# Scans two at a time in odd steps, the sums of squares moved behind the output part of step 1

## What is computed

```python
xn = layernorm(x)
gate, xBC, dt = split(xn @ in_proj_w.T, [8192, 8192 + 10240])      # 128 heads of 64
xBC = silu(causal_conv4(xBC) + conv_b)
xs, B, C = split(xBC)                                              # 8 groups of 16 heads
dt = clip(softplus(dt + dt_bias), 0.001, 100)
y = ssd(xs, B, C, D, dt)     # chunks of 128: (C B^T * exp(cs_l - cs_s) masked) @ (xs dt) + xs D
yg = y * silu(gate)
out = yg * rsqrt(mean_over_group(yg**2) + eps) * norm_w
s = out @ out_proj_w.T
g = silu(moe(xn))            # 16 experts of 56, top 2
return x + s * g
```

## Time and profile before

| | |
|---|---|
| median of 3 runs | 1604.44 us |
| the profiled execution, its own time | 1603.83 us |
| its span | 1602.0 us |
| TensorE's granted clock | 0.999 of full |
| busy PE, DVE, ACT, POOL | 1587.9, 1406.6, 1199.9, 959.6 us |

### The profile page before, as it was taken

How to read it: one execution, slowest core, us unless ns; L and a number is a source line. 1 busy time by engine, 2 the same in 40 slices (tenths; PEclk the granted TensorE clock), 3 DMA queues, 4 the chain that set the end, 5 groups by cost and what they waited for, 6 DMA issues and landing times.

```text
span 1602.0 us, 28468 instructions
## 1 busy us (share of the span) xinstructions
PE 1587.9 (99%) x8478; PEld 1266.6 (79%) x8478; DVE 1406.6 (88%) x1654; ACT 1199.9 (75%) x2309; POOL 959.6 (60%) x600
## 2 busy tenths in 40 slices
PE   9999999999999999999999999999999999999998
PEld 6888777887778777887778777887778777877776
DVE  7727899889999899889999899889998899889987
ACT  5525878777787878777787878777887878778772
POOL 6522466655666656655666556655666566656563
PEclk9999999999999999999999999999999999999999
DMA  5234344334443344334443334334433334334432
GB/s 188 80 131 150 127 138 169 115 132 142 146 146 112 128 137 165 118 131 143 141 146 117 127 130 168 122 130 144 145 141 119 126 129 166 126 120 152 152 132 86
DMA packets 83832, 216.89 MB, mean 135 GB/s; under 512 B 10576, under 2 KB 12880, under 8 KB 83536
## 3 DMA queue, kind: packets, MB, share of 16 engines
q1 hardware_dynamic: 83376, 214.55, 39.3%
q10 hardware_dynamic: 288, 0.30, 0.1%
HBM read 209.83 MB, written 4.98 MB: 134 GB/s over the span
## 4 chain that ended last, share of the span: by engine, by line
PE 84%; DVE 7%; ACT 4%; issue 3%; POOL 1%; DMA 0%; ACTq 0%; DVEq 0%; POOLq 0%
PE pj L455 15%; PE pj L457 14%; PE pj L456 14%; PE pr L455 9%; PE pr L456 8%; PE pr L457 7%; PE sc L702 7%; PE sc L706 3%; PE tb L691 3%; DVE conv L1394 3%; ACT decay L984 1%; DVE decay L1422 1%; DVE xc L1408 1%; DVE wo_lo L1458 1%; PE pr L680 1%
## 5 line engine op out<-in xcount | busy, mean ns | idle before, releaser
L1096 POOL TENSOR_TENSOR w_lo<-stg,w_hi 128x512 fp32r<-128x512 f32 x316 | 494.9, 1567 | 315.1 <-ACT w_hi L958 254.4
L455 PE MATMUL pj<-xT_hi,w_hi 128*128 128x512 f32 x1208 | 476.5, 394 | 3.6 <-POOL w_lo L1096 1.5
L457 PE MATMUL pj<-xT_hi,w_lo 128*128 128x512 f32 x1208 | 470.8, 390 | 0.0
L456 PE MATMUL pj<-xT_lo,w_hi 128*128 128x512 f32 x1208 | 470.4, 389 | 0.0
L1394 DVE SCALAR_TENSOR_TENSOR conv<-pj,par,conv 128x510 f32<-128x510 f32 (+2 forms) x480 | 357.8, 745 | 77.0 <-ACT conv L966 63.6
L984 ACT ACTIVATE decay<-decay,dtg 128x256 f32<-128x256 f32 (+1 forms) x1024 | 379.0, 442 | 0.0
L1137 POOL TENSOR_TENSOR xc<-xc,thg 128x512 f32<-128x512 f32 x128 | 203.1, 1587 | 188.9 <-DVE xc L1445 188.6
L1143 POOL TENSOR_TENSOR sqsum<-sqsum,sq 128x512 f32<-128x512 f32 x112 | 216.7, 1935 | 115.4 <-ACT sq L1012 112.1
L455 PEld LDWEIGHTS pj<-xT_hi,w_hi 128*128 128x128 f32 x1208 | 226.7, 188 | 58.8 <-issue 8.5
L457 PEld LDWEIGHTS pj<-xT_hi,w_lo 128*128 128x128 f32 x1208 | 226.7, 188 | 48.2
L456 PEld LDWEIGHTS pj<-xT_lo,w_hi 128*128 128x128 f32 x1208 | 226.9, 188 | 45.3
(11 more groups left out here) (185 smaller groups left out, 1976.4 us busy)
## 6 DMA issues: line engine op xcount, KB each, us to landing
stg<-wstream SPq DMA_DIRECT2D x387, 256.0 KB, 2.7
decay<-cs_scr SPq DMA_DIRECT2D x128, 768.0 KB, 4.3
acc<-hid SPq DMA_DIRECT2D x8, 256.0 KB, 5.0
out<-acc SPq DMA_DIRECT2D x8, 256.0 KB, 2.0
dt_scr<-decay SPq DMA_DIRECT2D x1, 1024.0 KB, 5.7
gate_scr<-part SPq DMA_DIRECT2D x4, 256.0 KB, 2.0
dtg<-dt_scr SPq DMA_DIRECT2D x16, 64.0 KB, 4.1
stg<-hid SPq DMA_DIRECT2D x4, 256.0 KB, 4.9
```

The lines of the kernel that those rows point to most:

```text
L455: nc.tensor.matmul(dst, hi_w, hi_x, start=first, stop=False)
L456: nc.tensor.matmul(dst, hi_w, lo_x, start=False, stop=False)
L457: return nc.tensor.matmul(dst, lo_w, hi_x, start=False, stop=last)
L1096: nc.gpsimd.tensor_tensor(w_dest(n, 1), stg[:, s % RING, :], f32(w_dest(n, 0)), ALU.subtract).then_inc(S["wl"], 1)
```

## The change

Each pair's scan used to stand in its own step. Now even steps hold none, and odd step s holds `scan(s-1)` and `scan(s)` next to each other; the transposes stay one per step. Each of the two needs a bank: pairs 0, 2, 4, 6 write `sc`; pair 1 writes `tb`, pair 3 `pr[0]`, pairs 5 and 7 `pr[3]`, with waits on those who used these banks last (`acc` of add_output, `u` of add_scan). The sums of squares go behind the output part of step 1, into `sc`, and the transposes of pair 2 go behind them. On VectorE both add_scans stand in the odd step, and both block_weights (s and s+1) and both y_lo in the even one; ScalarE's y_hi and square go in twos in even steps, its drops and decays are for s+1 and no longer for s+2; GpSimd does all weight splits of a step first, then the squares, and both `gated` in odd steps. SyncE issues the exponents of two pairs in even steps.

```diff
@@ banks
...
+        yb = [sc, tb, sc, pr[0], sc, pr[3], sc, pr[3]]
@@ SyncE, step
 def step(g, half, s):
...
-    if has_pair(g, half, s + 3):
-        load_exponents(*pair(g, half, s + 3))
+    for n in (s + 2, s + 3):
+        if s % 2 == 0 and has_pair(g, half, n):
+            load_exponents(*pair(g, half, n))
@@ TensorE
 def x_turn(g, half, j):
...
-    pe.wait_ge(S["ms"], at(g, half, 1, 0 if j >= 2 else -1))
...
+    if j == 2:
+        pe.wait_ge(S["u"], at(g, half, NJ, 2))
@@ TensorE, scan
 def scan(g, half, j):
...
-    pe.wait_ge(S["u"], at(g, half, NJ, j))
+    pe.wait_ge(S["u"], at(g, half, NJ, j - 1))
+    if j == 2:
+        pe.wait_ge(S["ms"], at(g, half, 1, 0))
+    if j > 1 and j % 2 == 1:
+        pe.wait_ge(S["acc"], at(g, half, 4, 1 if j == 3 else 4))
+    if j == 5:
+        pe.wait_ge(S["fg"], NTT)
...
-            nc.tensor.matmul(sc[hd, c0:c0 + 2 * P], xdt[:, j % 2, 2 * b, hd],
+            nc.tensor.matmul(yb[j][hd, c0:c0 + 2 * P], xdt[:, j % 2, 2 * b, hd],
...
-            mm = nc.tensor.matmul(sc[hd, c0 + P:c0 + 2 * P], xdt[:, j % 2, 2 * b + 1, hd],
+            mm = nc.tensor.matmul(yb[j][hd, c0 + P:c0 + 2 * P], xdt[:, j % 2, 2 * b + 1, hd],
...
 def square_sums(g, half):
...
-    pe.wait_ge(S["xdt"], at(g, half, NJ, 0 if isinstance(g, int) and g == G else 2))
+    if isinstance(g, int) and g == G:
+        pe.wait_ge(S["xdt"], at(g, half, NJ, 0))
+        dst = tb
+    else:
+        pe.wait_ge(S["u"], at(g, half, NJ, 1))
+        dst = sc
...
-        mm = nc.tensor.matmul(tb[:, t:t + 1], sqsum[:, t * P:(t + 1) * P], ones, start=True, stop=True)
+        mm = nc.tensor.matmul(dst[:, t:t + 1], sqsum[:, t * P:(t + 1) * P], ones, start=True, stop=True)
@@ TensorE, out_first
...
+    if t in (0, 3):
+        pe.wait_ge(S["u"], at(g, half, NJ, 4 if t == 0 else NJ))
@@ TensorE, step
...
-    if s == 1 and with_out:
-        square_sums(g, half)
...
-    if has_pair(g, half, s + 1):
+    if s != 1 and has_pair(g, half, s + 1):
         x_turn(*pair(g, half, s + 1))
-    if has_pair(g, half, s):
+    if s % 2 == 1 and has_pair(g, half, s):
+        scan(g, half, s - 1)
         scan(g, half, s)
...
     if with_out:
         out_of_step(g, half, s)
+    if s == 1 and with_out:
+        square_sums(g, half)
+    if s == 1:
+        x_turn(*pair(g, half, s + 1))
@@ ScalarE, step
...
 def step(g, half, s, with_out=True):
...
+    before = (g, 0) if half == 1 else (g - 1, 1)
...
+    gated = ("g", s) in blocks(g, half, s)
+    mine = [b[1] for b in blocks(g, half, s) if b[0] == "x"]
+    todo = list(range(len(pieces(g, half, s))))
+    raised = has_pair(g, half, s + 1)
+    done = []
+    if s == 0 and with_out:
+        done = [(*before, NJ - 2), (*before, NJ - 1)]
+    elif s >= 2 and s % 2 == 0 and has_pair(g, half, s - 1):
+        done = [(g, half, s - 2), (g, half, s - 1)]
+    if gated and todo:
+        split(g, half, s, todo.pop(0))
+    if raised and not fill:
+        drops(*pair(g, half, s + 1), 0)
+    if gated:
         gate_tanh(g, half, s)
...
+    if done:
+        y_hi(*done[0])
+    if mine:
+        tap(g, half, mine[0])
+    if todo:
+        split(g, half, s, todo.pop(0))
     if fill and s == 4:
         expert_hi(13)
...
+    if done:
+        y_hi(*done[1])
+        square(*done[0])
+    if raised and fill:
+        drops(*pair(g, half, s + 1), 0)
+    if raised:
+        drops(*pair(g, half, s + 1), 1)
+    if raised and s % 2 == 1:
+        decays(*pair(g, half, s + 1))
...
+        x_tanh(*of_half(g, half, mine[0]), mine[0])
+    for m in mine[1:]:
+        tap(g, half, m)
+    if todo:
+        split(g, half, s, todo.pop(0))
+    if raised and s % 2 == 0:
+        decays(*pair(g, half, s + 1))
+    for m in mine[1:]:
+        x_tanh(*of_half(g, half, m), m)
+    if done:
+        square(*done[1])
+    while todo:
+        split(g, half, s, todo.pop(0))
@@ ScalarE, the end
...
-y_hi(G - 1, 1, NJ - 1)
-square(G - 1, 1, NJ - 1)
+for j in (NJ - 2, NJ - 1):
+    y_hi(G - 1, 1, j)
+    square(G - 1, 1, j)
@@ GpSimd, step
...
-    if with_out and s == 0:
-        add_square(*before, NJ - 1)
+    for i in range(1, n):
+        split_low(g, half, s, i)
     if with_out and s == 2:
         inverse_rms(*before)
-    if s >= 2 and has_pair(g, half, s):
+    if s >= 4 and s % 2 == 0 and has_pair(g, half, s):
+        add_square(g, half, s - 2)
+    if with_out and s == 0:
+        add_square(*before, NJ - 2)
+        add_square(*before, NJ - 1)
+    if s >= 2 and s % 2 == 0 and has_pair(g, half, s):
...
-    for i in range(1, n):
-        split_low(g, half, s, i)
-    if has_pair(g, half, s):
+    if s % 2 == 1 and has_pair(g, half, s):
+        gated(g, half, s - 1)
@@ GpSimd, the end
...
+add_square(G - 1, 1, NJ - 2)
@@ VectorE, add_scan
...
-                                   in1=sc[:, :], op0=ALU.mult, op1=ALU.add).then_inc(S["u"], 1)
+                                   in1=yb[j][:, :], op0=ALU.mult, op1=ALU.add).then_inc(S["u"], 1)
@@ VectorE
 def mean_square(g, half):
...
-    nc.vector.tensor_scalar(msq[:, :], tb[:, 0:4], 1.0 / (GH * HD), 4.0 * EPS, ALU.mult, ALU.add
+    sums = tb if is_last(g, half) else sc
+    nc.vector.tensor_scalar(msq[:, :], sums[:, 0:4], 1.0 / (GH * HD), 4.0 * EPS, ALU.mult, ALU.add
@@ VectorE, step
 def step(g, half, s, with_out=True):
...
+    fill = isinstance(g, int) and g < 0
...
+    even = s % 2 == 0
+    done = []
+    if s == 0 and with_out:
+        done = [(*before, NJ - 2), (*before, NJ - 1)]
+    elif s >= 2 and even and has_pair(g, half, s - 1):
+        done = [(g, half, s - 2), (g, half, s - 1)]
...
     if half == 1 and s == 4 and not isinstance(g, int):
         conv_parameters(g + 1)
...
+    if with_out and s == 2:
...
+    if with_out and s == 5:
+        add_output(*before, 3)
     if has_pair(g, half, s):
         gate_silu(g, half, s)
...
+    if mine:
...
+    if fill and s == 4:
         expert_weighted(13)
     if s == 5 and not is_last(g, half):
         mask_products(*following(g, half))
...
+    if even and has_pair(g, half, s + 1):
         x_times_dt(*pair(g, half, s + 1))
...
+    if not even and has_pair(g, half, s):
+        add_scan(g, half, s - 1)
         add_scan(g, half, s)
+    if not even and s != 1 and has_pair(g, half, s + 1):
+        x_times_dt(*pair(g, half, s + 1))
+    if even and has_pair(g, half, s):
+        block_weights(g, half, s)
...
+    if fill and s == 4:
         expert_lo(13)
...
+    if done:
+        y_lo(*done[0])
     if mine:
         x_silu(*of_half(g, half, mine[0]), mine[0])
...
+    if even and s != 4 and has_pair(g, half, s + 1):
+        block_weights(g, half, s + 1)
+    for m in mine[1:]:
+        x_silu(*of_half(g, half, m), m)
+    if with_out and 3 <= s <= 4:
+        add_output(*before, s - 2)
+    if not fill:
         split_out_lo(g, half, s)
...
+    if s == 4 and has_pair(g, half, s + 1):
+        block_weights(g, half, s + 1)
+    if with_out and s == 2:
+        add_output(*before, 0)
+    if s == 1 and has_pair(g, half, s + 1):
+        x_times_dt(*pair(g, half, s + 1))
+    if done:
+        y_lo(*done[1])
@@ VectorE, the end
...
+y_lo(G - 1, 1, NJ - 2)
+finish(4)
...
-finish(4)
...
```

More of the change, by code:

```diff
@@ L1014, in step @@
             def step(g, half, s, with_out=True):
-                mine = [b for b in blocks(g, half, s) if b[0] == "x"]
-                n = len(pieces(g, half, s))
-                i = 0
+                before = (g, 0) if half == 1 else (g - 1, 1)
                 fill = isinstance(g, int) and g < 0
[L1019 to L1026, removed]
-                    if has_pair(g, half, s + 2):
-                        drops(*pair(g, half, s + 2), 0)
-                    gate_tanh(g, half, s)
-                elif has_pair(g, half, s + 2):
-                    drops(*pair(g, half, s + 2), 0)
@@ L1032, in step @@
-                if s >= 1 and has_pair(g, half, s - 1):
-                    y_hi(g, half, s - 1)
-                    square(g, half, s - 1)
-                if s == 0 and with_out:
-                    before = (g, 0) if half == 1 else (g - 1, 1)
-                    y_hi(*before, NJ - 1)
-                    square(*before, NJ - 1)
-                if has_pair(g, half, s + 2):
-                    drops(*pair(g, half, s + 2), 1)
-                if mine and not (fill and s == NJ - 1):
-                    tap(g, half, mine[0][1])
@@ L1043, in step @@
-                if i < n:
-                    split(g, half, s, i)
-                    i += 1
+                gated = ("g", s) in blocks(g, half, s)
[7 more added lines that the diff above has]
+                    done = [(g, half, s - 2), (g, half, s - 1)]
@@ L1046, in step @@
+                if gated and todo:
[3 more added lines that the diff above has]
+                if gated:
+                    gate_tanh(g, half, s)
+                if done:
[4 more added lines that the diff above has]
+                    split(g, half, s, todo.pop(0))
                 if fill and s == 4:
                     expert_hi(13)
```

(51 more changed lines are left out.)

2 lines of the change are left out of this document (removed).

## The result

The changed kernel takes 1646.64 us (median of 4 runs, 1643.4 to 1650.15), the kernel before 1605.26 us beside it (1604.13 to 1606.73). The ratio is 1.0257, 95% interval 1.0243 to 1.027: 2.6% slower, where 0.7% faster was forecast. The profiled execution has a span of 1643.5 us, 41.5 more than before.

What follows compares the result with a forecast made beforehand. TensorE, busy 99% of the span, was taken to set the time. From 1603.8 us, 23 us of gross gain off and 12 us of new waits for VectorE added gave 1592.8, stated as 1592.5; range 1580 to 1608.

Steps and rivals of the forecast that it cites:

- The gross gain, 23 us: TensorE: scans in twos save 21.8 us over 64 pairs of steps, moved sums of squares 1.2; together about 23.
- the sum without waits: Rival "no new waits": all of VectorE's room holds and TensorE never waits; 1581, up to 1585 us; chance 0.22.
- The rival on the switch: TensorE's second scan pays as the first does: 9.6 us less gain, 1602 with waits, no change; chance 0.10.
- I cost both at nothing: SyncE's two pairs of exponents in even steps, and piece loads queued behind them, needed a step later: 0 us.
- the forecast's net gain of 11: Whole kernel: 23 us gross gain less 12 us of waits, 1603.8 to 1592.8 us.
- Waits for VectorE, 12 us with a bound of 33: TensorE waiting at scans of pairs 3 and 5 after VectorE-GpSimd collisions: 0.8 us a half, 12 in all; bounds 0 and 33.
- Pair 5 was to wait in half 0: scan(5) behind add_output(3): TensorE's 14.5 us against VectorE's 13.6, room 0.9; one and a half collisions overrun it by 0.75.
- split_out_lo was costed at 0.66: VectorE's split_out_lo, start to start, 0.66 us in the sums of room for pairs 3 and 5.
- the room of 0.9: Pair 3, half 0: TensorE's 10.5 us against VectorE's 9.6; one collision of 1.1 overruns it by 0.2.
- out_second(0) for y_lo(7): 0.1 to 0.3 allowed: Remaining waits, such as y_lo(7) ahead of out_second in half 1 and exp of s+1: 0.1 to 0.3 us.
- 0 to 1.5 us allowed for the last step: Kernel's end: y_hi, square and y_lo of two pairs behind the last scans, the first covered by 24 products; 0 to 1.5 us.
- VectorE becomes the bound: Rival: scan(5) and scan(3) wait for add_output after collisions, 2.0 us a half, 31 us, 1612, slower; chance 0.16.

Runs made afterwards that it cites:

- tiny_squares: Changed kernel with exponents of one pair loaded each step and GpSimd's add_square cut to 4 of 512 columns, so squares are not summed: 1581.65 us, 0.9853.
- one_load: Changed kernel with SyncE loading the exponents of one pair (s+2) in each step instead of two pairs in even steps: 1624.06 us, 1.0126.
- late_finish: Changed kernel with VectorE's calls of `finish` in the last step moved behind what TensorE waits for: 1641.2 us, 1.0222.
- squares_before_splits: Changed kernel with one load a step and the first of an even step's two add_squares back ahead of the later weight splits on GpSimd: 1658.2 us, 1.0331.

## Why the prediction was wrong, step by step

**The gross gain, 23 us: right.** Transposes to scan 0.53, two scans 2.75, transposes to products 0.35, sums of squares 0.81 (in tiny_squares, where they don't wait): each within 0.02 of its term, but for the transposes behind the sums of squares, 0.39 and not 0.36. The second scan costs 1.30, not 1.45. tiny_squares ends at 1581.65, where the sum without waits gave 1581, and its loop gains 2.9 us an iteration. The rival on the switch falls.

**"I cost both at nothing", of the exponents' loads: the step that failed most.** The prediction asked who needs the data and found room of a step. It did not ask what else goes through the same DMA engines at that time: the loop ends in step 4, an even one, right behind the loads, and the packets of code that the branch waits for are on nobody's list of instructions. The term is 22.6 us (one_load), by itself more than the forecast's net gain of 11. With it at 22.6 and nothing else changed, the sum would have been 1615, slower. It could have been read from the trace of before: six branches of 3.9 to 4.3 us with 0.4 us uncovered each, so that nothing was left there to give.

**Waits for VectorE, 12 us with a bound of 33: mis-sized.** one_load against tiny_squares gives 42 us: 3.5 for each iteration of the loop, and 15 behind it. The mechanism was right: collisions with GpSimd lengthen block_weights and y_lo by 1.1 each, and the squares are the cause. The Trainium skill, page SBUF — State Buffer, section SBUF: two separate sides, calls the port pair an exclusive lock; the rows agree: a y_lo of 0.68 becomes 1.76, and the ends of both rows add up as turns. Five errors made up the size.

- Places. The largest recurring wait, Q for add_scan(0), 15 x 0.67 = 10 us, isn't among the deadlines at all, though the diff shows it, `pe.wait_ge(S["u"], at(g, half, NJ, 1))`. I had costed Q on TensorE alone and took "behind the output part" for late enough. VectorE, with the taps of the gate block ahead of add_scan(0), is later.
- Which half. Pair 5 was to wait in half 0, with split_out_lo. In the loop it waits in half 1, 7 x 0.63, and in half 0 never. In half 1 a square is followed by two splits in a row, onto block_weights and y_lo; in half 0 of one_load split_out_lo stands between, GpSimd idles for its next weight, and block_weights stays at 1.74 us. Room added up from durations didn't tell where the collisions fall.
- split_out_lo was costed at 0.66 from the one undisturbed row. The list of lines of the kernel before, below, has a mean of 1650 ns for it. In pair 3's stretch of half 0 it takes 1.77 in the changed kernel (559.09), and that one meeting uses up the room of 0.9: the scan waits 0.42.
- out_second(0) for y_lo(7): 0.1 to 0.3 allowed, 0.71 measured, and again only in half 1.
- The ends. 0 to 1.5 us allowed for the last step; it lost 6.0 to waits and 3.4 to the clock, because `finish` twice stands ahead of what TensorE needs (late_finish takes 4.9 of the 6.0 away) and because the squares lengthen what is queued there (without them 2.5 of the 6.0 stay). I counted the y_lo's and not what is queued between them. The first and the last group lose another 8.1, of which 1.1 stay without the squares.

```profile
L1458 DVE SCALAR_TENSOR_TENSOR wo_lo<-stg,par,wo_hi 128x512 fp32r<-128x512 f32 x64 | 105.6, 1650 | 0.0
```

**The clock: missing.** No term stood for it. Before, the clock was 0.999 over the span; after, six drops to 1.2 GHz cost 11.9 us. A sum of waits is too low where waits are long: the 13 new us of waits at the loop ends came with 22.6 us of time.

**"What would show it".** Idle time ahead of the scans of steps 3 and 5, released by VectorE, is there, as named. Of the signs against the forecast, longer rows of block_weights came (mean 1.95 us, 1.88 before), while x_silu's grew shorter. The waits at channel blocks named as a sign against the forecast are there too, at six places; the name of their releaser in the list, conv, is wrong, and the sequencer's records show the branch.

**The rivals.** "VectorE becomes the bound" has the sign, at 1612 by scan(5) and scan(3); these two cost 7 us in the loop, not 31. The time came from causes that no rival held.

## What to carry to other kernels

When transfers are moved, ask what stands behind them on the DMA engines and not only who needs them: here the branch at the loop's end waited there for its code, with its cover all used. When an operation comes to be awaited, sum its engine's queue up to it with every collision counted full, and write down each new wait of the diff as a deadline, the small ones too. A cause that is taken away tells a size best: leaving the squares out showed 42 us, where one_load's list of TensorE's waits for VectorE adds up to some 34, 5 of which stay.

## What the runs showed of the hardware

- The taken branch at the loop's end costs TensorE's sequencer 3.3 to 5.0 us with up to 768 KB queued shortly ahead (48 branches of eight kernels) and 5.3 to 7.1 with 1.5 MB (30 of five). The time up to the instruction packet grows with the traffic, from 0.9 to 2.6 us to 3.0 to 4.8. No trace here shows it with an idle DMA.
- A single wait of 1.5 to 3.4 us at a loop end came with a drop to 1.2 GHz (0.7 us ahead of the wait's end to 1.3 behind it) in 21 of 30 cases in the five kernels that have such waits, for 3.4 us in 19 and for 6.8 in two; waits of 1.3 us and less at loop ends never did. The wait's length doesn't separate them: 2.83 was once with and once without a drop, 1.97 with one, 3.4 without.
- A wait's cost is not its length alone: behind one the second product comes 0.33 us after the first, not 0.23.
- VectorE and GpSimd lengthen each other by turns: VectorE's 0.68 becomes 1.76, and GpSimd's 1.30 becomes 1.75 to 2.9. A queue of two operations on GpSimd therefore holds VectorE up twice, and in squares_before_splits another order of the same operations on GpSimd cost 34 us.
